# Attention layers over a counted graph: a layer's first chunk beside the last chunk's steps of the one before

## The reference

```python
h = x @ W
a, b = h @ a_src, h @ a_dst                    # one number per node each
e = leaky_relu(a[src] + b[dst], 0.2)           # one per edge
ex = exp(e - segment_max(e, dst)[dst])
out = segment_sum(ex / segment_sum(ex, dst)[dst] * h[src], dst) + bias
```

## Time and profile before

| | us |
|---|---|
| median of three runs (812.20 to 815.85) | 815.23 |
| profiled execution, its own time | 810.32 |
| its span, first to last instruction | 808.6 |
| busy: TensorE, VectorE | 677.2 (84%), 720.8 (89%) |
| busy: ScalarE, GpSimd | 524.4 (65%), 299.4 (37%) |
| mean granted clock of TensorE | 0.918 of full speed |

### The profile page before, as it was taken

The page is one execution under the profiler, slowest core; times in us unless marked ns, Lnnn a source line. Parts: engine busy times, 40 slices in busy tenths (PEclk is TensorE's granted clock), DMA queues, the critical chain, the costliest instruction groups (busy, mean ns, idle before and its releaser), DMA issues.

```text
span 808.6 us, 14270 instructions
## 1 busy us (share of the span) xinstructions
PE 677.2 (84%) x5705; PEld 657.9 (81%) x5705; DVE 720.8 (89%) x975; ACT 524.4 (65%) x826; POOL 299.4 (37%) x237
## 2 busy tenths in 40 slices
PE   4345988898978999999976989899993899898893
PEld 4345888898878999999975989899892899898893
DVE  5499999999959999999945999999993999999993
ACT  0053444434459987887835989788772998687680
POOL 1504000000014554544511546557461357474562
PEclk9996888788887999999996999999996799999997
DMA  3400000000000000000000000000000000110001
GB/s 98 109 0 1 1 2 1 1 1 1 2 0 18 17 1 17 17 2 1 1 4 17 1 17 16 2 17 1 1 1 3 17 17 2 32 32 2 17 3 34
DMA packets 11204, 10.63 MB, mean 13 GB/s; under 512 B 2258, under 2 KB 9295, under 8 KB 11120
## 3 DMA queue, kind: packets, MB, share of 16 engines
q1 hardware_dynamic: 10320, 8.27, 3.4%
q0 software_dynamic: 800, 1.26, 0.6%
HBM read 7.89 MB, written 1.64 MB: 12 GB/s over the span
## 4 chain that ended last, share of the span: by engine, by line
DVE 51%; PE 32%; issue 11%; DMA 2%; ACT 2%; POOL 1%; DVEq 0%; POOLq 0%; ACTq 0%
DVE ps L818 18%; PE ps L1401 17%; DVE scratch L656 14%; DVE scratch L946 10%; PE ps L1305 7%; DVE ps L821 3%; PE ps L1265 2%; PE ps L1457 1%; PE ps L1436 1%; DVE mu L834 1%; DMA edge_sb<-in_edges 1%; PE ps L1312 1%; DVE scratch L818 1%; PE ps L1410 1%; DMA gathered<-in_edges,start_i 1%
## 5 line engine op out<-in xcount | busy, mean ns | idle before, releaser
L507 POOL TENSOR_TENSOR scratch<-scratch 125x625 f32<-125x625 f32 x165 | 229.3, 1394 | 239.9 <-ACT scratch L1189 239.8
L1401 PE MATMUL ps<-hA,scratch 125*125 125x129 f32 x2300 | 272.8, 279 | 18.9 <-DVE scratch L946 16.5
L1401 PEld LDWEIGHTS ps<-hA,scratch 125*125 125x125 f32 x2300 | 265.0, 192 | 24.2 <-DVE scratch L946 21.5
L818 DVE SCALAR_TENSOR_TENSOR ps<-C,a_unit,ps 125x625 f32<-125x625 uint8 x330 | 278.9, 866 | 1.9
L946 DVE SCALAR_TENSOR_TENSOR scratch<-ps,r_src,C 125x625 f32<-125x625 f32 x210 | 180.7, 860 | 3.7 <-PE ps L1384 3.7
L1305 PE MATMUL ps<-scratch 128*128 128x125 bf16 x1250 | 148.4, 296 | 23.3 <-DVE scratch L656 17.1
L1305 PEld LDWEIGHTS ps<-scratch 128*128 128x128 bf16 x1250 | 143.1, 121 | 27.6 <-DVE scratch L656 21.1
L1184 ACT ACTIVATE scratch<-gathered,r_inv 125x625 f32<-125x625 f32 x165 | 133.2, 807 | 28.2 <-PE ps L1401 28.1
L1189 ACT ACTIVATE scratch<-scratch,r_src 125x625 f32<-125x625 f32 x165 | 147.8, 896 | 0.0
L1401 PE MATMUL ps<-hB,scratch 125*125 125x129 f32 x1150 | 136.4, 277 | 13.4 <-DVE scratch L946 11.3
L1401 PEld LDWEIGHTS ps<-hB,scratch 125*125 125x125 f32 x1150 | 131.0, 189 | 17.9 <-DVE scratch L946 15.1
(11 more groups left out here) (155 smaller groups left out, 493.6 us busy)
## 6 DMA issues: line engine op xcount, KB each, us to landing
gathered<-g_lines SPq DMA_DIRECT2D x12, 305.2 KB
xr<-in_x SPq DMA_DIRECT2D x1, 1562.5 KB
out<-xr SPq DMA_DIRECT2D x5, 312.5 KB
edge_sb<-in_edges SPq DMA_DIRECT2D x1, 805.7 KB
w<-in_W SPq DMA_DIRECT2D x2, 128.0 KB
gathered<-in_edges,start_i POOLq DMA_INDIRECT x5, 6.2
w<-in_W SPq DMA_DIRECT2D x1, 64.0 KB
av<-in_a_src SPq DMA_DIRECT2D x4, 0.5 KB
```

Of the source, the lines that this page charges most:

```text
L507: g.tensor_tensor(A, A, wide[n % 2], ALU.mult).then_inc(pool_done[L], 1)
L818: v.scalar_tensor_tensor(dest, counts, a_unit[:, s:s + 1], top, ALU.min, ALU.max).then_inc(top_done[L], 1)
L1401: last = mm(ps[0:P, acc_at(t):acc_at(t) + HW], A[:, P * t:P * (t + 1)], feat, start=opens and t in (0, 3), stop=closes, skip_group_check=True)
```

## The change

The chunks are numbered through, q = 0 to 14. Chunks 5 and 10 ("turn" chunks) start beside the steps of chunks 4 and 9.

- A layer's extremes are first taken from its first 15 tiles (EARLY_TILES), which are known one chunk earlier, in the last chunk of the preceding layer. The range is widened by half its width on each side; `a_unit` is over a fixed span of 100. The extremes of tiles 15 to 24 are taken in the turn chunk and compared with the widened range at its end (`set_mode`), which then sets `fast` for going on.
- Exponentials, cuts, units and reciprocals come in parts (tiles 0 to 14, 15 to 19, 20 to 24) with two buffers each. The scalars run on GpSimd.
- In the turn chunk the preceding chunk's steps come earlier (TURN), maxima of tiles 20 to 24 at steps 21 to 23.
- New features always go to `hA`; `scale_features` writes the scaled copy to `hB3`, when the last chunk has used the tile.
- `g_row` goes to memory straight from its column form, as 4-byte elements (`write_lines`), not by a transpose, a copy and a store of rows.
- The last result is added on VectorE in one step per tile to an x that already holds the bias.
- If a mode fails, the engines leave the nested Ifs, and the careful program computes all three layers anew at the end, in place of the Else branches.

```diff
+        EARLY_TILES = 15
+        LATE = 20
+        At = namedtuple("At", "tops chain kappa z stats pool pe act rest_pe rest_act")
+        USUAL = (At(1, (3, 4, 5, 6), 6, (8, 9, 10), None, (14,), (12, 15, 21), (14, 17, 23), 18, 20),
+                 At(1, (3, 4, 5, 6), 6, (8, 9, 10), (13, 14), (14, 19), (18, None, 21), (16, 20, 23), None, None),
...
+        BEFORE_LAST = (At(1, (3, 4, 5, 6), 6, (8, 9, 10), None, (14,), (12, 14, 19), (13, 16, 21), 17, 18),
...
+        TURN = (At(None, (1, 1, 2, 2), 3, (4, 5, 6), None, (11,), (8, 10, 15), (9, 12, 17), 12, 13),
+                At(None, (1, 1, 2, 2), 3, (4, 5, 6), (9, 10), (11, 15), (15, None, 18), (13, 16, 19), None, None))
...
+        def top_at(q, k):
+            if turn(q) and k >= LATE:
+                return (21, 21, 22, 22, 23)[k - LATE]
+            return (k - AHEAD) * (T - 3) // (T - 1 - AHEAD)
+        def pass_at(q, s):
+            if turn(q) and s >= LATE:
+                return q * T + 20 + (s - LATE) // 2
+            return q * T + s - PASS_AHEAD
...
 # SyncE
+            def write_lines(L, t0, t1):
+                sp.wait_ge(g_done, LINES[L, t0])
+                sp.dma_start(g_d[L, t0 * P:t1 * P].rearrange("(t p) -> p t", p=P), g_row[L % 2][:, t0:t1],
+                             allow_slow_non_contiguous=True).then_inc(lines_stored, 16)
...
+                    ga_load(L * NC + 4)
+                    if L < LAYERS - 1:
+                        write_lines(L + 1, 0, EARLY_TILES)
+                        ga_load((L + 1) * NC)
+                        ga_load((L + 1) * NC + 1)
+                        layer(L + 1)
...
 # GpSimd, chunk(q)
+                    if c == NC - 1 and L < LAYERS - 1:
+                        if s == 7:
+                            extremes(L + 1)
+                            scalars(L + 1)
+                        if s == 9:
+                            cuts(L + 1, 0, EARLY_TILES)
+                            units(L + 1, 0, EARLY_TILES)
+                            backs(L + 1, 0, EARLY_TILES, 2 * L + 1)
+                    if turn(q):
+                        if s == 3:
+                            pool.wait_ge(F.new_sb, q - 1)
+                            units(L, EARLY_TILES, LATE)
+                        if s == 21:
+                            pool.wait_ge(F.new_sb, q)
+                            cuts(L, EARLY_TILES, T)
+                            units(L, LATE, T)
+                            backs(L, EARLY_TILES, T, 2 * L)
+                        if s == T:
+                            pool.wait_ge(ext_all_ready, L)
+                            g.partition_all_reduce(ext_all[:, :], ext[:, :], P, MAX_OVER_PARTITIONS).then_inc(all_ready, 1)
...
 # VectorE
+            def extremes_late(L):
+                dve.wait_ge(F.new_sb, L * NC)
+                dve.wait_ge(extg_ready, L + 1)
+                extremes(L, EARLY_TILES, T)
...
+            def set_mode(L):
+                if L:
+                    dve.wait_ge(all_ready, L)
+                    v.tensor_scalar(within[:, 0:1], ext_all[:, 0:1], wide_ext[L % 2][:, 0:1], covers[:, :], ALU.is_le,
+                                    ALU.mult).then_inc(within_lin, 1)
...
+                    if c == NC - 1 and L < LAYERS - 1:
+                        if s == 1:
+                            extremes_early(L + 1)
+                        if s == 10:
+                            inverse_r(L + 1, 0, EARLY_TILES)
+                    if turn(q):
+                        if s == 5:
+                            inverse_r(L, EARLY_TILES, LATE)
+                        if s == 19:
+                            extremes_late(L)
+                        if s == LATE:
+                            inverse_r(L, LATE, T)
+                if turn(q):
+                    set_mode(L)
+                if q < Q - 1:
+                    for k in range(AHEAD):
+                        next_top(q + 1, k)
...
+            def last_result():
+                for t in range(CT):
+                    xt = xr[:, (NC - 1) * CT + t, :]
+                    last = v.scalar_tensor_tensor(xt, raw[:, t, 0:D], rz[:, t:t + 1], xt, ALU.mult, ALU.add)
...
 # ScalarE, chunk(q)
+                    if c == NC - 1 and L < LAYERS - 1:
+                        if s == 7:
+                            exps_dst(L + 1, 0, EARLY_TILES)
+                            exps_src(L + 1, 0, EARLY_TILES)
+                        if 9 <= s < 9 + EARLY_TILES:
+                            scale_features(L + 1, s - 9)
+                        if s == T - 1:
+                            act.wait_ge(F.new_sb, q)
+                            exps_src(L + 1, EARLY_TILES, LATE)
+                    if turn(q):
+                        if s < LATE - EARLY_TILES:
+                            scale_features(L, EARLY_TILES + s)
+                        if s == post_at(q).act[2]:
+                            act.wait_ge(F.new_sb, q)
+                            exps_src(L, LATE, T)
+                            for t in range(LATE, T):
+                                scale_features(L, t)
+                        if s == 22:
+                            exps_dst(L, EARLY_TILES, T)
...
 # every engine
+            def layer(L):
+                if L:
+                    chunk(L * NC)
+                pe.wait_ge(mode_ready, L + 1)
+                with pe.If(pe.value_load(fast[0:1, L:L + 1], min_val=0, max_val=1)):
+                    for c in range(1 if L else 0, NC):
+                        chunk(L * NC + c)
+                    if L < LAYERS - 1:
+                        layer(L + 1)
```

## The result

The kernel after takes 824.87 us (median of 4 runs, 823.39 to 825.67), the kernel before 813.72 (4 runs beside it, 811.18 to 815.85): ratio 1.0136, with a 95% interval of [1.0098, 1.0174]; such brackets stand behind each ratio below. The forecast of 790.4 lies on the wrong side. In the profiled executions the span grew from 808.6 to 823.5 us.

The account below looks back on a forecast made before the run. Chunks bound by DVE (PE in layer 0), two turns by a chain of waits. -14.1 - 8.8 + 1.0 - 2.9 = -24.8 from the profiled 810.32 gives 785.5, plus 4.9 to the runs' median: 790.4 us; range 775 to 804.

Parts of the forecast that it names:

- POOL takes over eighteen small operations per turn [...] and one more all-reduce of 0.4: GpSimd at each turn: 4.5 us of small operations plus 0.4, covered by its idle time; without cover 4.9 us a turn.
- Turn 1, -14.1: Layer 0's last product to first product of layer 1's second chunk: 47.6 us against 61.67.
- turn 2, -8.8: Layer 1's last product to first product of layer 2's second chunk: 50.4 us against 59.20.
- Rival A: Turns: new features come out before DVE reaches step 19, so it never stands; 776.4 us, chance 0.20.
- POOL's all-reduce 0.4: End of the turn's chunk: 0.4 us within the 8.7 us chain from `new_sb`, against 7.9 for DVE's large steps.
- ScalarE in the last chunk, +1.0 in layer 1 and 0 in layer 0: Added scaled tiles and exponentials fill ScalarE to 32.5 of 34.2 us: +1.0 in layer 1; PE covers it in layer 0.
- rival B: Last and turn chunks: ScalarE becomes the bound, +12 to +17 us on the forecast, 803 to 807 us; chance 0.18.
- 4-byte stores, 0: `g_row` stores as 4-byte elements: early one takes 2.8 to 11.5 us within a 15.8 us window, hidden, cost 0.
- Rival C: Early `g_row` store not hidden beyond 42 ns a packet, delaying a new layer's row maxima; chance 0.07, 0.05 of it slower.
- Start of layer 0, between 0 and -1.6, taken as 0: Some 1.6 us of scalars leave DVE between two one-hot steps; taken as 0 since PE must finish counts there.
- The tail, -2.9: After the last inverse, five DVE products-with-addition of 1.40 us replace POOL's scaling and additions: -2.9 us.
- Rival D: Late tiles' extremes fall outside the widened range and the careful program also runs, some 870 us more; chance 0.01.

Follow-up runs that it names:

- the copies: Kernel after, with the four GpSimd all-reduces of layers 1 and 2 replaced by GpSimd copies, leaving out the maximum over partitions: 793.30 us.
- the PE maximum: Kernel after, each turn's two reductions over partitions on PE and VectorE: 803.87 us; with copy earlier, GpSimd scalars later, layer 0's scalars on VectorE: 791.72 us.

## Why the prediction was wrong, by its steps

- **The step that failed** is "POOL takes over eighteen small operations per turn [...] and one more all-reduce of 0.4", covered since GpSimd was busy for only 17.39 of 29.00 us. The small operations cost what I said (0.18 to 0.41 us each, 12 in the last chunk). The all-reduce was priced by its busy time, 0.4. It costs some 13 us of GpSimd in a last chunk and some 18 at the end of a turn's chunk (with the If on the mode that follows it there), and copies in place of the four in layers 1 and 2 gave 31.6 us. Even the price without that cover, 4.9 us a turn, was an underbid: 15.8 us a turn. A busy share over 29 us was also the wrong cover for it: of stops of 13.1 to 13.6 us the chunks hid only 5 to 9. I read this as the lead of GpSimd's products over their readers, since one is wanted every second tile; the lead itself was not measured. The 11.6 us of idle time in the chunk lie in many pieces.
- The way in could not be read from the trace before, the way back could at least have been suspected: the all-reduce stood alone in a hole on each turn, with 8.97 and 8.90 us behind it.
- **Turn 1, -14.1, and turn 2, -8.8.** Right in their chains once the stop is gone: 12.8 and 10.5 us with the copies, 12.8 and 8.2 with the PE maximum (table). DVE's wait for `new_sb`, forecast at 5 and 6 us, is 5.58 and 5.34. Rival A (no standing) is ruled out by it.
- **"POOL's all-reduce 0.4"** also stood in the turn's closing chain of 8.7 us, which I set against DVE's 7.9. With 5.85 us ahead of it, DVE waits 6.17 and 6.49 us for `ext_all`.
- **ScalarE in the last chunk, +1.0 in layer 1 and 0 in layer 0:** chunks 9 and 4 grew by 1.9 and 1.4 us with the copies, and the cause named was the wrong one. The time is VectorE's: it was busy throughout chunk 4 before and is so with the copies, and its busy time grew by the same 1.44 us, while ScalarE has 3 us free. In layer 0 PE covers nothing: VectorE is as full there as PE. So the work added to VectorE in the last chunk, put at 0.8 and counted at turn 2 alone, belonged in both layers. It is far from rival B; ScalarE stood 44.7 us for GpSimd's products in the kernel after, which is not lack of its time.

Chunk 4 before, then with the copies (stretch, its length, then busy us of PE, PEld, DVE, ACT and POOL):

```profile
381.45:410.49 29.04, 28.52 (x257) 28.19 (x256) 29.00 (x42) 24.01 (x37) 15.27 (x11) 1.00 0.01 1
```

```profile
384.45:414.93 30.48, 28.56 (x252) 27.77 (x251) 30.44 (x47) 27.30 (x51) 17.85 (x24) 1.00 0.11 15
```

- **4-byte stores, 0:** right. The early store was issued at 405.7 us and the load behind it at 412.8, so it took at most 7.1 us, inside the 2.8 to 11.5 us, and no row maximum of a new layer waited for a DMA. The view of DMA from 405 to 412 us has 1880 packets in 25.1% of 16 engines' time, 15 ns each, and for most of the store 4 to 5 tenths of that time were busy, where I had put five engines of 16. Rival C falls; its decisive price was 42 ns.
- **Start of layer 0, between 0 and -1.6, taken as 0:** +2.8, by the way back from layer 0's all-reduce (shown by moving the scalars). I had looked only at what leaves DVE and not at where it goes.
- **The tail, -2.9:** -2.5 in the trace, -2.0 as a part by itself.
- **Rival D:** as forecast, the careful program did not run; the time has no room for its some 870 us.
- **The sum, -24.8, without the failed step** is too large by some 5 to 6 us: the span shrank by 19.6 us with the copies and by 18.8 with the PE maximum. With the PE maximum chunks 4 and 9 are 2.7 and 1.9 us longer than before, where I had 0 and 1.0, and the turns gave 21.0 us of 22.9. That 790.4 lies beside 791.7 is luck: it was taken from a median of 815.23 for the kernel before, and beside the experiments that kernel took 811.53 to 812.26. Why turn 2 is 2.3 us longer with the PE maximum than with the copies was not tried.

## What to carry to other kernels

A busy time prices an instruction only if the trace shows its neighbours close up; where it always stands alone in a hole, ask what the hole covers before moving it into a full stage. For an all-reduce over partitions on GpSimd, the one such instruction seen here, look at the gap on both sides, put down to "issue", and if it must move, group all of them (two in a row paid once) or do the same work on another engine. An engine's idle share over a chunk is not the cover for one long stop: of 11.6 us idle, 5 to 9 us of a stop were hidden. And when a forecast comes out near a mended kernel's time, compare the changes against the kernel before measured beside it, not the two totals.

## What the runs showed of the hardware that I had not expected

- An all-reduce among ordinary instructions stops GpSimd for 5.75 to 6.26 us before it (18 cases in the traces) and 6.86 to 7.70 us behind it (17 cases with no If behind it), though it takes 0.37 (2.03 the first time, in layer 0). Where the If on the mode follows, the gap is 8.5 to 9.5 us in the kernel before and 11.0 to 11.6 after; how it is made up was not tried. A second one directly behind it takes 0.43 and nothing more. On an engine that idles for its input the way in disappears (433.16 in the trace before: the result came 0.46 us after DVE began to wait), the way back does not (6.96 us in layer 0).
- Some small DVE operations between SBUF tiles do not end before a GpSimd product that is running: `e_top`, 686.55 + 1.03 = 687.58 beside 686.04 + 1.52 = 687.56, against 0.15 alone, and `back` in the same way. It does not hold for all: a reciprocal of the same 125 by 5 elements, with one tile as input, keeps its 0.17 to 0.19 us and ends 0.7 to 1.3 us before the product beside it, eight times in the trace of the version at 791.7. DVE's large products, which read one of their tiles from PSUM, keep their 0.86 us beside them. The Trainium skill, SBUF — State Buffer, § Who interferes with whom, has one pair of ports shared by the two engines under an exclusive lock, and the rows of `e_top` agree. Moving one such operation only moved the meeting to the next.

A reciprocal on DVE that ends first, and the product on GpSimd beside it:

```profile
658.49 0.19 DVE L932 RECIPROCAL zk<-zk 125x5 f32<-125x5 f32 x1
```

```profile
658.42 1.52 POOL L579 TENSOR_TENSOR scratch<-scratch 125x625 f32<-125x625 f32 x1 [2.55 <-ACT scratch L1374]
```
